# State input product on two column tiles, and the second FP4 quantiser over both token tiles at once

## The chip, the cores and the metric

One Trainium2 chip (trn2), one NeuronCore. The metric is the device time of one launch in microseconds (us), the median of three runs. PE is TensorE, ACT is ScalarE, DVE is VectorE, POOL is GpSimd, SP is SyncE, which issues most transfers here.

## The reference

A residual stream x of 16 sequences of 256 tokens with 128 channels goes through four stages: gated linear attention, a mixture of 8 experts, a state space block, and a feed-forward block with FP4 quantised products. The change touches the last two.

```
# state space block: D_INNER 256, D_STATE 16
xc = silu(conv(xp) + conv_b)
h  = 0.9 * h + 0.1 * (xt @ w_B)          # along the tokens
y  = (h @ w_C) * silu(z);  x = x + y @ w_out
# FP4 block, H 128, I 352, blocks of 16 along the last axis
scale = max(|block|) / 6;  q = nearest grid value of block / scale, times scale
x = x + fp4(silu(fp4(x) @ gate) * (fp4(x) @ up)) @ down
```

## The kernel before, in words

Four phases follow one another: `phase_a` (attention), `phase_b` (router and scatter), `phase_c` (experts, and the preparation of the weights of the last phase), `phase_d` (state space block and FP4 block).

`phase_c` starts with two loads of rows, then SP waits for two memsets of POOL (L1236), issues the loads of the weights (L1240 to L1249) and only then, in order on the same engine, the load of the third group of rows (L1221, in `run_skewed`).

`phase_d` works on one sequence (256 tokens, two token tiles of 128) at a time, in a software pipeline. `body(j)` of each engine holds pieces of several sequences: a = j+3 (projection, convolution, state input, scan), b = j+2 (state output, first FP4 quantiser), c = j+1 (gate and up products, hidden values, second quantiser to its step 4), d = j (last step of the second quantiser, its rescale, the down product), e = j+4 (layer norm). The order on each engine is written by hand, and semaphores join them. Passes j = 0 to 12 have all the sequences a to d; `body` runs from j = -4 to 15, with the passes 1 to 10 in a hardware loop of two passes a turn.

What touches the change, in the order of a pass:

- PE multiplies 128 rows of w_C by the states `hs` (L1744, "state output"), transposes, multiplies `yz` by w_out (L1763), makes the gate and up products, transposes `hq` of token tile 0 into ps_H and of tile 1 into ps_Y (L1788), and then makes the convolution product ps_A (L1796 by the helper's lines 188 to 190) and ps_Z. Then comes the state input product (L1807), `xs` by w_B, two accumulating FP32 matmuls of 128 rows by 16 columns, into ps_M[0:16]; then the down product ps_G (L1816).
- ACT makes `xs` (L1580, two halves), the magnitudes of the second quantiser (L1586, whose operation is at L899; two of 352 elements), `zs` (L1590), the magnitude of the first quantiser (L1593, also L899; 256 elements), and `us` (L1597), the copy of the state input out of PSUM.
- DVE makes step 4 of the second quantiser (L920, `d_fh_sum`, one for each token tile), step 4 of the first (L920, `d_fx_sum`), the scan (L1712) over `us` into `hs`, and later `yz` (L1663), then step 5 of the second quantiser (L921, `d_fh_v`). Steps 0 to 3 (L911 to L917) come in the same pass as the hidden values `hid` (L1691), with the two token tiles taken in turn at each step.
- POOL rescales the two token tiles (L1523, the operation at L895), each as soon as step 5 of its tile is done, and then works out the sums of two layer norms (L1508 to L1515) and gathers rows (L1493).

The class `Fp4` (L876) holds the quantiser's steps: 0 maximum of each block, 1 scale, 2 reciprocal, 3 divide, 4 and 5 rounding by a large constant. `DS` is 16, `N` 256, `F` 352, `P` 128.

Of the kernel before, what the change touches and what calls it, by code (L numbers as in the profile page):

```python
# [28 lines left out]
P = 128  # L29
# [99 lines left out]
def build(nc, io, out):  # L129
    ctx = ExitStack()  # L130
    with ctx:
# [21 lines left out]
        with ExitStack() as mid:  # L153
# [9 lines left out]
            with ExitStack() as early:  # L163
# [14 lines left out]
                "wb": sbm("wb", [P, 2, DS]),  # L178
# [697 lines left out]
class Fp4:  # L876
# [15 lines left out]

    def rescale(self, eng, to):

        return eng.tensor_tensor(self.by(to), self.by(self.v[:, :]), self.spread(self.scale), ALU.mult)  # L895
# [277 lines left out]
def phase_c(nc, io, g):  # L1173
# [3 lines left out]
    with ExitStack() as ctx:  # L1177
# [40 lines left out]
        def _(sp):  # L1218
# [17 lines left out]
            sp.wait_ge(s_zero, 2)  # L1236
# [10 lines left out]
            sp.dma_start(g["wb"][:, :, :], io["L1_attn_w_B"].rearrange("(b p) s -> p b s", p=P)).then_inc(s_w, 16)  # L1247
            sp.dma_start(g["wout"][:, :, :], io["L1_attn_w_out"].rearrange("(b p) s -> p b s", p=P)).then_inc(s_w, 16)
            sp.dma_start(g["wc"][0:DS, :], io["L1_attn_w_C"]).then_inc(s_w, 16)  # L1249
# [3 lines left out]
            sp.wait_ge(s_w, 16 * 7)  # L1253

        @blk_.gpsimd
        def _(pool):
            nc.gpsimd.memset(wraw[:, 2 * D:6 * D], 0.0).then_inc(s_zero, 1)
            nc.gpsimd.memset(g["wc"][:, :], 0.0).then_inc(s_zero, 1)

            pool.wait_ge(s_w, 16 * 7)  # L1260
# [136 lines left out]
def phase_d(nc, io, g, out):  # L1397
# [6 lines left out]
    with ExitStack() as ctx:  # L1404
# [9 lines left out]
        decay = sb("decay", [DS, N])  # L1414
# [11 lines left out]
        us = sb("us", [DS, N])  # L1426
# [10 lines left out]
        hid = sb("hid", [P, 2, F])  # L1437
        hq = sb("hq", [P, 2, F])
        hqT = sb("hqT", [P, 2, 3, P])
        fp4_x = Fp4(nc, sb, "fx", 2 * D)  # L1440
        fp4_h = [Fp4(nc, sb, f"fh{t}", F) for t in range(2)]
# [47 lines left out]
        def _(pool):  # L1489
# [27 lines left out]
            def body(j):  # L1517
                b, d, e = j + 2, j, j + 4
                if live(d):
                    for t in range(2):  # L1520
                        wait(pool, s_qh, d, n=t + 1, per=2)
                        wait(pool, s_hp, d, n=t + 1, per=2, ago=1)
                        fp4_h[t].rescale(nc.gpsimd, hq[:, t, :]).then_inc(s_hq, 1)  # L1523
# [11 lines left out]
        def _(act):  # L1535
# [10 lines left out]
            def body(j):  # L1546
# [35 lines left out]
                if live(c):  # L1582
                    for t in range(2):
                        act.wait_ge(s_qz, c.lin(10, 7 + t))
                        wait(act, s_qh, c, n=t + 1, per=2, ago=1)
                        fp4_h[t].magnitude().then_inc(s_mag, 1)  # L1586
# [7 lines left out]
                if live(a):  # L1594
                    wait(act, s_u, a)
                    wait(act, s_scan, a, ago=1)
                    nc.scalar.activation(us[:, :], ps_M[0:DS, 0:N], ACT.Copy, scale=0.1).then_inc(s_us, 1)  # L1597
# [11 lines left out]
        def _(dve):  # L1609
# [4 lines left out]
            PER = 10  # L1614
# [15 lines left out]
            def hidden_step(c, n, t):  # L1630

                if n == 0:
                    wait(dve, s_h, c, n=t + 1, per=2)
                elif n == 4:
                    wait(dve, s_mag, c, n=t + 1, per=2)
                else:
                    if n == 1:
                        wait(dve, s_hq, c, n=t + 1, per=2, ago=1)
                    dve.wait_ge(s_qz, c.lin(PER, 2 * n - 1 + t))
                fp4_h[t].step(n, hid[:, t, :]).then_inc(s_qz if n < 5 else s_qh, 1)  # L1640
# [16 lines left out]
            def body(j):  # L1657
# [18 lines left out]
                if live(d):  # L1676
                    for t in range(2):
# [169 lines left out]
```

## Time and profile before

| | us |
|---|---|
| median of 3 runs | 649.71 |
| lowest and highest of them | 648.31, 651.97 |
| the profiled execution | 653.99 |
| its span | 652.3 |
| `phase_c`, from its first load to the last product, about | 308 to 415 |
| `phase_d`, about | 419 to 652 |
| PE, DVE, POOL, ACT busy, share of the span | 85%, 67%, 54%, 47% |

The profile is of one execution, whose time is 1.7 us above its span (start and end) and 4.3 us above the median of the runs. Busy time is what an engine spent in instructions; the rows below name an engine, the line in the kernel, the operation, and what goes out and in.

### The profile page before, as it was taken

The numbers are of one execution on the slowest core, as the hardware profiler recorded it, in microseconds if no ns is written. First come the engines' busy times: TensorE is split into PE (matmuls) and PEld (weight loads), VectorE is DVE, ScalarE is ACT, GpSimd is POOL, SyncE is SP. The second block draws the span as 40 slices with busy tenths as digits, with TensorE's granted clock in tenths as the row PEclk, the third lists the DMA queues.
The fourth block names the chain that finished last, engine by engine and source line by source line (L and its number), as shares of the span: only waits on it lengthen the run. The fifth ranks groups of instructions, "written<-read, shape, count | busy, mean of one in ns | idle before, by whom it ended". The sixth has DMA issues, their size and how long they took to land. (4 is left out here: it accounts for less than half of the span.)

```text
span 652.3 us, 15280 instructions
## 1 busy us (share of the span) xinstructions
PE 551.6 (85%) x4468; PEld 445.9 (68%) x4469; DVE 438.3 (67%) x1172; ACT 307.8 (47%) x862; POOL 355.2 (54%) x550
## 2 busy tenths in 40 slices
PE   2799999999999379991799999278899999999965
PEld 1457676776776258871689999266778778778754
DVE  2678999999885155552284343126899899899883
ACT  1356666666574224430245444124545645655632
POOL 4468877878776248885400000445667767764221
PEclk9999999999999659996699999778899999999987
DMA  7000000000004551111422111110011011010000
GB/s 200 16 20 33 19 26 25 16 32 16 23 26 108 158 196 34 32 34 43 116 58 57 56 56 40 33 16 10 10 32 18 16 32 17 16 25 15 10 17 16
DMA packets 41686, 28.12 MB, mean 43 GB/s; under 512 B 5232, under 2 KB 38192, under 8 KB 41648
## 3 DMA queue, kind: packets, MB, share of 16 engines
q1 hardware_dynamic: 36016, 23.46, 12.2%
q0 software_dynamic: 5632, 4.20, 3.7%
q8 instruction: 19, 0.31, 0.2%
q14 instruction: 19, 0.16, 0.1%
HBM read 14.01 MB, written 9.44 MB: 36 GB/s over the span
## 5 line engine op out<-in xcount | busy, mean ns | idle before, releaser
L821 PE MATMUL a_ps_a<-a_qx,a_kt 32*128 32x512 f32 x512 | 70.8, 643 | 1.2 <-DMA a_qx<-a_qs 1.0
L1493 POOL DMA_INDIRECT x<-yg_dram,pos x32 | 58.1, 1815 | 11.9 <-issue 11.9
L895 POOL TENSOR_TENSOR d_hq<-d_fh_v,d_fh_scale 128x352 f32<-128x352 f32 x32 | 27.9, 889 | 57.6 <-DVE d_fh_v L921 57.6
L361 POOL TENSOR_SCALAR_AFFINE_SELECT a_at<-a_at 128x512 f32<-128x512 f32 x80 | 50.5, 650 | 11.8 <-ACT a_at L423 11.5
L1317 DVE TENSOR_TENSOR c_hid<-c_act,c_ps 128x352 f32<-128x352 f32 x40 | 20.7, 520 | 44.4 <-ACT c_act L1274 35.7
L423 ACT ACTIVATE a_at<-a_ps_a 128x512 f32<-128x512 f32 x80 | 44.5, 600 | 11.7 <-PE a_ps_a L821 10.1
L1498 POOL MEMSET d_hs<- 128x256 f32 x1 | 0.3, 311 | 88.3 <-POOLq L1177 88.3
L821 PEld LDWEIGHTS a_ps_a<-a_qx,a_kt 32*128 32x128 f32 x512 | 32.1, 192 | 17.9 <-issue 17.2
L1274 ACT ACTIVATE c_act<-c_ps 128x352 f32<-128x352 f32 x40 | 18.5, 463 | 49.6 <-PE c_ps L190 49.2
L1002 POOL DMA_INDIRECT xg_dram<-xn,pos x32 | 35.3, 1104 | 11.9 <-DVE pos L1091 6.2
L188 PE MATMUL d_ps_A<-d_xnT,wmix 128*128 128x256 f32 x128 | 38.4, 300 | 1.6 <-DVE d_xnT L1672 0.9
L540 DVE TENSOR_TENSOR a_at<-a_ps_a,mask 128x512 f32<-128x512 f32 x48 | 32.7, 684 | 8.6 <-PE a_ps_a L821 7.3
L190 PE MATMUL d_ps_A<-d_xnT,wmix 128*128 128x256 f32 x128 | 37.2, 290 | 0.0
L189 PE MATMUL d_ps_A<-d_xnT,wmix 128*128 128x256 f32 x128 | 37.2, 290 | 0.0
L745 PE MATMUL a_ps_o<-a_at,a_vpad 128*32 128x128 f32 x1024 | 34.6, 276 | 0.0
L1107 DVE TENSOR_TENSOR b_hid<-b_act,b_ps 128x512 f32<-128x512 f32 (+1 forms) x24 | 16.4, 683 | 25.8 <-ACT b_act L1032 25.8
L188 PE MATMUL c_ps<-w13p,c_xT 128*128 x80 | 30.8, 385 | 2.0 <-issue 1.0
L1032 ACT ACTIVATE b_act<-b_ps 128x512 f32<-128x512 f32 (+1 forms) x24 | 14.3, 596 | 38.4 <-PE b_ps L190 37.9
L1367 PE MATMUL c_ps_y<-w,c_hidT 128*128 (+1 forms) x240 | 31.6, 281 | 0.8 <-ACT c_hidT L1291 0.8
L393 POOL TENSOR_TENSOR a_kt<-a_e,a_rope 128x512 f32<-128x512 f32 x16 | 20.4, 1276 | 21.6 <-ACT a_e L447 21.6
L1367 PEld LDWEIGHTS c_ps_y<-w,c_hidT 128*128 128x128 f32 (+1 forms) x240 | 28.3, 191 | 3.0 <-issue 1.9
L1816 PEld LDWEIGHTS d_ps_G<-d_wd,d_hqT 128*128 128x128 f32 (+1 forms) x192 | 23.8, 199 | 8.6 <-issue 5.5
(274 smaller groups left out, 1807.3 us busy)
## 6 DMA issues: line engine op xcount, KB each, us to landing
a_qx<-a_qs SPq DMA_DIRECT2D x64, 64.0 KB, 1.9
b_w<-in_L_ffn_w_eDF_dram SPq DMA_DIRECT2D x2, 1408.0 KB, 8.1
xg_dram<-a_zero SPq DMA_DIRECT2D x40, 64.0 KB, 1.6
c_rows<-xg_dram SPq DMA_DIRECT2D x20, 128.0 KB, 2.1
yg_dram<-c_y SPq DMA_DIRECT2D x20, 128.0 KB, 1.8
out_dram<-x SPq DMA_DIRECT2D x16, 128.0 KB, 1.9
w<-in_L_ffn_w_eFD_dram SPq DMA_DIRECT2D x2, 512.0 KB, 5.1
x<-in_L_attn_x_dram SPq DMA_DIRECT2D x1, 768.0 KB, 5.7
```

What stands on the lines that cost most here:

```text
L188: nc.tensor.matmul(to, left(0), right(0), start=start, stop=False)
L189: nc.tensor.matmul(to, left(0), right(1), start=False, stop=False)
L190: return nc.tensor.matmul(to, left(1), right(0), start=False, stop=stop)
L361: nc.gpsimd.affine_select(at[:, t, r, :, :], at[:, t, r, :, :], pattern=[[0, 4], [1, P]], compare_op=ALU.is_ge, fill=0.0, base=0, channel_ ...
L423: nc.scalar.activation(at[:, t, r, :, :], ps_a[:, r, :, :], ACT.Copy).then_inc(s_copied, 1)
L540: nc.vector.tensor_tensor(at[:, t, r, :, :], ps_a[:, r, :, :], mask[:, 0:1, :].to_broadcast([P, 4, P]), ALU.mult).then_inc(s_masked, 1)
L745: last = nc.tensor.matmul(ps_o[32 * r:32 * r + 32, tile(t)], vpad[:, b.par, t, c0:c0 + 32], at[:, t, r, h, :], start=(t == 0 and h == 0), ...
L821: last = nc.tensor.matmul(ps_a[:, r, :, :], kt[rows, b.par, c_, tile(t)], qx[rows, b.par, :, c_, tile(t)], start=(c_ == 0), stop=(c_ == 1))
L895: return eng.tensor_tensor(self.by(to), self.by(self.v[:, :]), self.spread(self.scale), ALU.mult)
L1002: nc.gpsimd.indirect_dma_start(out=g["xg_dram"][:, :], out_offset=bass.IndirectOffsetOnAxis(ap=g["pos"][:, t:t + 1], axis=0), in_=xn2[:, t ...
L1367: last = nc.tensor.matmul(ps_y[:, t, :], hidT[0:fn, f.par, t, n, :], w2[0:fn, e_out[t], n, :], start=(n == 0), stop=(n == 2))
L1493: nc.gpsimd.indirect_dma_start(out=x[:, t, :], out_offset=None, in_=g["yg_dram"][:, :], in_offset=bass.IndirectOffsetOnAxis(ap=g["pos"][:, ...
```

## The change

The state input product no longer accumulates its two halves of 128 inner channels in the same 16 rows of PSUM. Each half gets its own column tile of the PE array: w_B is kept in 32 columns, of which 16 are zeros, and the halves go to ps_M[0:32] and ps_M[32:64]. `us`, `decay` and the scan work on 64 partitions instead of 16, and w_C stands twice in `wc` (rows 0 to 15 and 32 to 47), so that the state output product adds the halves. For that one more memset on POOL and one more load on SP stand in `phase_c`.

The second quantiser (`fp4_h`) is one of 704 elements instead of two of 352: each of its steps 0 to 5 is one DVE instruction, and its magnitude one ACT instruction. The rescale on POOL stays in two instructions of 352, but both now wait for the one step 5.

```
-                "wb": sbm("wb", [P, 2, DS]),
+                "wb": sbm("wb", [P, 2, 2 * DS]),
...
+    def rescale_part(self, eng, to, c0, c1):
+
+        return eng.tensor_tensor(self.by(to[:, c0:c1]), self.by(self.v[:, c0:c1]),
+                                 self.scale[:, c0 // QB:c1 // QB].unsqueeze(2).to_broadcast([P, (c1 - c0) // QB, QB]), ALU.mult)
...
-            sp.wait_ge(s_zero, 2)
+            sp.wait_ge(s_zero, 3)
...
-            sp.dma_start(g["wb"][:, :, :], io["L1_attn_w_B"].rearrange("(b p) s -> p b s", p=P)).then_inc(s_w, 16)
+            sp.dma_start(g["wb"][:, :, 0:DS], io["L1_attn_w_B"].rearrange("(b p) s -> p b s", p=P)).then_inc(s_w, 16)
             sp.dma_start(g["wout"][:, :, :], io["L1_attn_w_out"].rearrange("(b p) s -> p b s", p=P)).then_inc(s_w, 16)
-            sp.dma_start(g["wc"][0:DS, :], io["L1_attn_w_C"]).then_inc(s_w, 16)
+            for h in range(2):
+                sp.dma_start(g["wc"][2 * DS * h:2 * DS * h + DS, :], io["L1_attn_w_C"]).then_inc(s_w, 16)
...
             nc.gpsimd.memset(g["wc"][:, :], 0.0).then_inc(s_zero, 1)
-
-            pool.wait_ge(s_w, 16 * 7)
+            nc.gpsimd.memset(g["wb"][:, :, :], 0.0).then_inc(s_zero, 1)
+
+            pool.wait_ge(s_w, 16 * 8)
...
-        decay = sb("decay", [DS, N])
+        decay = sb("decay", [4 * DS, N])
...
-        us = sb("us", [DS, N])
+        us = sb("us", [4 * DS, N])
...
-        fp4_h = [Fp4(nc, sb, f"fh{t}", F) for t in range(2)]
+        fp4_h = Fp4(nc, sb, "fh", 2 * F)
...
                 if live(d):
+                    wait(pool, s_qh, d)
                     for t in range(2):
-                        wait(pool, s_qh, d, n=t + 1, per=2)
                         wait(pool, s_hp, d, n=t + 1, per=2, ago=1)
-                        fp4_h[t].rescale(nc.gpsimd, hq[:, t, :]).then_inc(s_hq, 1)
+                        fp4_h.rescale_part(nc.gpsimd, hq, F * t, F * t + F).then_inc(s_hq, 1)
...
                 if live(c):
-                    for t in range(2):
-                        act.wait_ge(s_qz, c.lin(10, 7 + t))
-                        wait(act, s_qh, c, n=t + 1, per=2, ago=1)
-                        fp4_h[t].magnitude().then_inc(s_mag, 1)
+                    act.wait_ge(s_qz, c.lin(5, 4))
+                    wait(act, s_qh, c, ago=1)
+                    fp4_h.magnitude().then_inc(s_mag, 1)
...
-                    nc.scalar.activation(us[:, :], ps_M[0:DS, 0:N], ACT.Copy, scale=0.1).then_inc(s_us, 1)
+                    nc.scalar.activation(us[:, :], ps_M[0:4 * DS, 0:N], ACT.Copy, scale=0.1).then_inc(s_us, 1)
...
-            def hidden_step(c, n, t):
+            def hidden_step(c, n):
 
                 if n == 0:
-                    wait(dve, s_h, c, n=t + 1, per=2)
+                    wait(dve, s_h, c, n=2, per=2)
                 elif n == 4:
-                    wait(dve, s_mag, c, n=t + 1, per=2)
+                    wait(dve, s_mag, c)
                 else:
                     if n == 1:
-                        wait(dve, s_hq, c, n=t + 1, per=2, ago=1)
-                    dve.wait_ge(s_qz, c.lin(PER, 2 * n - 1 + t))
-                fp4_h[t].step(n, hid[:, t, :]).then_inc(s_qz if n < 5 else s_qh, 1)
+                        wait(dve, s_hq, c, n=2, per=2, ago=1)
+                    dve.wait_ge(s_qz, c.lin(5, n))
+                fp4_h.step(n, hid[:, :]).then_inc(s_qz if n < 5 else s_qh, 1)
...
                     for n in range(4):
-                        for t in range(2):
-                            hidden_step(c, n, t)
+                        hidden_step(c, n)
...
-                    nc.vector.tensor_tensor_scan(hs[0:DS, :], decay[:, :], us[:, :], 0.0, ALU.mult, ALU.add).then_inc(s_scan, 1)
+                    nc.vector.tensor_tensor_scan(hs[0:4 * DS, :], decay[:, :], us[:, :], 0.0, ALU.mult, ALU.add).then_inc(s_scan, 1)
...
                     for h in range(2):
-                        last = nc.tensor.matmul(ps_M[0:DS, 0:N], wb[:, h, :], xs[:, h, :], start=(h == 0), stop=(h == 1))
+                        r0 = 2 * DS * h
+                        last = nc.tensor.matmul(ps_M[r0:r0 + 2 * DS, 0:N], wb[:, h, :], xs[:, h, :], start=True, stop=True)
                     last.then_inc(s_u, 1)
```

## Rows read from the trace of the kernel before

**Rows 1.** Page, part 1: busy time, share of the span, instructions.

```profile
PE 551.6 (85%) x4468; PEld 445.9 (68%) x4469; DVE 438.3 (67%) x1172; ACT 307.8 (47%) x862; POOL 355.2 (54%) x550
```

**Rows 2.** Stretches of the last phase: busy us of PE, PEld, DVE, ACT, POOL; clock.

```profile
544.40:618.30 73.90, 69.92 (x481) 59.76 (x481) 67.21 (x206) 40.80 (x115) 41.86 (x64) 1.00 0.10 18
618.30:633.00 14.70, 9.44 (x61) 7.72 (x62) 12.86 (x36) 6.15 (x17) 3.06 (x6) 0.92 0.03 10
```

**Rows 3.** Timeline of PEld in one pass: start, us, idle before and releaser.

```profile
510.09 0.73 PEld L1744 LDWEIGHTS d_ps_Y<-d_hs,wc 128*128 128x128 f32 x4 [0.23 <-DVE d_hs L1712]
...
515.35 0.30 PEld L1788 LDWEIGHTS d_ps_Y<-mask,d_hq 128*128 128x128 f32 x3 [0.19 <-POOL d_hq L895]
```

**Rows 4.** Waits between 475 and 615 us: total, times, longest.

```profile
PEld d_ps_Y L1788 <- POOL d_hq L895: 2.5, 11, 0.3
```

**Rows 5.** Timeline of PE in the same pass.

```profile
507.48 1.04 PE L1807 MATMUL d_ps_M<-d_xs,wb 128*16 128x256 f32 x4 [0.22 <-ACT d_xs L1580]
```

**Rows 6.** Timeline of ACT in the same pass.

```profile
506.59 0.84 ACT L1580 ACTIVATE d_xs<-d_ps_A,cb 128x256 f32<-128x256 f32 x2 [0.52 <-PE d_ps_A L190]
507.32 0.88 ACT L899 ACTIVATE d_fh_k<-d_fh_v 128x352 f32<-128x352 f32 x2
508.09 0.59 ACT L1590 ACTIVATE d_zs<-d_ps_Z 128x512 f32<-128x512 f32 x1
508.57 0.42 ACT L899 ACTIVATE d_fx_k<-d_fx_v 128x256 f32<-128x256 f32 x1
508.88 0.36 ACT L1597 ACTIVATE d_us<-d_ps_M 16x256 f32<-16x256 f32 x1
```

**Rows 7.** Timeline of DVE in the same pass.

```profile
505.31 0.93 DVE L917 SCALAR_TENSOR_TENSOR d_fh_v<-d_hid,d_fh_inv 128x352 f32<-128x352 f32 x2
...
507.85 0.96 DVE L920 SCALAR_TENSOR_TENSOR d_fh_sum<-d_fh_k,d_fh_v 128x352 f32<-128x352 f32 x2 [0.32 <-ACT d_fh_k L899]
509.02 0.42 DVE L920 SCALAR_TENSOR_TENSOR d_fx_sum<-d_fx_k,d_fx_v 128x256 f32<-128x256 f32 x1 [0.22 <-ACT d_fx_k L899]
509.36 0.67 DVE L1712 TENSOR_TENSOR_SCAN d_hs<-d_decay,d_us 16x256 f32<-16x256 f32 x1
...
512.96 0.94 DVE L921 SCALAR_TENSOR_TENSOR d_fh_v<-d_fh_k,d_fh_sum 128x352 f32<-128x352 f32 x2
```

**Rows 8.** Groups of the last phase by line: count, busy us, mean ns.

```profile
L921 DVE SCALAR_TENSOR_TENSOR d_fh_v<-d_fh_k,d_fh_sum 128x352 f32<-128x352 f32 x32 | 15.1, 513 | 0.0
```

**Rows 9.** Timeline of POOL in the same pass.

```profile
503.69 0.72 POOL L1510 TENSOR_TENSOR d_rstd<-d_rstd,halves 128x2 f32<-128x2 f32 x1
...
505.42 0.96 POOL L1510 TENSOR_TENSOR d_rstd<-d_rstd,halves 128x2 f32<-128x2 f32 x1
...
513.55 1.74 POOL L895 TENSOR_TENSOR d_hq<-d_fh_v,d_fh_scale 128x352 f32<-128x352 f32 x2 [1.76 <-DVE d_fh_v L921]
```

**Rows 10.** The rescales on POOL by tile: shortest, median, longest ns.

```profile
L895 POOL TENSOR_TENSOR d_hq<-d_fh_v,d_fh_scale x32: 777/889/1002, 463.7 to 644.3; 128x352 f32<-128x352 f32 x32
```

**Rows 11.** Page, part 5: a product of the first phase on four column tiles.

```profile
L745 PE MATMUL a_ps_o<-a_at,a_vpad 128*32 128x128 f32 x1024 | 34.6, 276 | 0.0
```

**Rows 12.** Timeline of SP at the start of the expert phase.

```profile
314.36 0.47 SPq L1248 DMA_DIRECT2D wout<-in_L_attn_w_out_dram  x1
314.87 0.47 SPq L1249 DMA_DIRECT2D wc<-in_L_attn_w_C_dram  x1
315.38 4.50 SPq L1221 DMA_DIRECT2D c_rows<-xg_dram  x3
```

**Rows 13.** Timeline of PE there.

```profile
319.04 0.44 PE L1359 MATMUL c_ps_t<-mask,c_rows 128*128 128x128 f32 x2 [2.67 <-DMA c_rows<-xg_dram]
```

**Rows 14.** Timeline of ACT in the first pass of the last phase.

```profile
434.65 0.37 ACT L1597 ACTIVATE d_us<-d_ps_M 16x256 f32<-16x256 f32 x1 [0.61 <-PE d_ps_M L1807]
```

**Rows 15.** Timeline of the last pass: the second quantiser of the last sequence.

```profile
640.43 0.93 DVE L917 SCALAR_TENSOR_TENSOR d_fh_v<-d_hid,d_fh_inv 128x352 f32<-128x352 f32 x2
640.96 0.93 ACT L899 ACTIVATE d_fh_k<-d_fh_v 128x352 f32<-128x352 f32 x2 [1.61 <-DVE d_fh_v L917]
641.49 0.96 DVE L920 SCALAR_TENSOR_TENSOR d_fh_sum<-d_fh_k,d_fh_v 128x352 f32<-128x352 f32 x2
...
643.29 1.74 POOL L895 TENSOR_TENSOR d_hq<-d_fh_v,d_fh_scale 128x352 f32<-128x352 f32 x2 [6.65 <-DVE d_fh_v L921]
```

More of the change, by code:

```diff
@@ L1252, in _ @@
                 sp.wait_ge(s_out[par], 16 * (PAIRS // 2))
-            sp.wait_ge(s_w, 16 * 7)
+            sp.wait_ge(s_w, 16 * 8)
         @blk_.gpsimd
@@ L1436, in phase_d @@
         silu = sb("silu", [P, 2, F])
-        hid = sb("hid", [P, 2, F])
-        hq = sb("hq", [P, 2, F])
+        hid = sb("hid", [P, 2 * F])
+        hq = sb("hq", [P, 2 * F])
         hqT = sb("hqT", [P, 2, 3, P])
         fp4_x = Fp4(nc, sb, "fx", 2 * D)
-        fp4_h = [Fp4(nc, sb, f"fh{t}", F) for t in range(2)]
+        fp4_h = Fp4(nc, sb, "fh", 2 * F)
         ps_T, ps_Y, ps_G, ps_U, ps_A, ps_Z, ps_H, ps_M = (bank("ps_" + n) for n in "TYGUAZHM")
@@ L1613, in _ @@
             dve.wait_ge(s_wz, 2)
-            PER = 10
             def norm_stats(j, st, s_stats, s_done):
@@ L1676, in body @@
                 if live(d):
-                    for t in range(2):
-                        hidden_step(d, 5, t)
+                    hidden_step(d, 5)
                 if live(b):
@@ L1690, in body @@
                         wait(dve, s_sg, c, n=t + 1, per=2)
-                        nc.vector.tensor_tensor(hid[:, t, :], silu[:, t, :], (ps_U, ps_Z)[t][:, 0:F], ALU.mult).then_inc(s_h, 1)
+                        nc.vector.tensor_tensor(hid[:, F * t:F * t + F], silu[:, t, :], (ps_U, ps_Z)[t][:, 0:F], ALU.mult).then_inc(s_h, 1)
                         if t == 0 and live(b):
@@ L1695, in body @@
                     for n in range(4):
-                        for t in range(2):
-                            hidden_step(c, n, t)
+                        hidden_step(c, n)
                 elif live(b):
@@ L1704, in body @@
                 if live(c):
-                    for t in range(2):
-                        hidden_step(c, 4, t)
+                    hidden_step(c, 4)
                 if live(b):
@@ L1787, in body @@
                         for f, (f0, fn) in enumerate(FT):
-                            last = nc.tensor.transpose(to[0:fn, P * f:P * f + P], hq[:, t, f0:f0 + fn], ident)
+                            last = nc.tensor.transpose(to[0:fn, P * f:P * f + P], hq[:, F * t + f0:F * t + f0 + fn], ident)
                         last.then_inc(s_hp, 1)
```

## The prediction, made blind

> **What bounds the kernel now.** I read the page first: PE is the busiest engine [rows 1]. Then the last phase by stretches. From 544.40 to 618.30 us six passes go by, 12.3 us each, with PE busy 69.92 of 73.90 us at the full clock [rows 2]. DVE is busy 67.21 us there, so both are nearly full, and what matters is which wait closes each piece of the loop. Two do. First, the state output product starts at 510.09 us, when the scan is done: its weight load had been idle 0.23 us for `d_hs` [rows 3]. Second, the transposes of `hq` of token tile 1 start at 515.35 us, 0.05 us after POOL's rescales end (513.55 + 1.74 = 515.29) [rows 3, 9], and this wait comes 11 times in the steady passes [rows 4]. So the loop runs: `yz` and DVE's queue, step 5 of the second quantiser, POOL's rescales, the transposes, the convolution product, `xs`, then ACT and DVE to the scan, then the state output product and `yz` again. The state input product is not in it: `xs` is done at 507.43 us, and from there ACT works without a gap through `d_fh_k`, `zs`, `d_fx_k` and `us` [rows 6]. The product, started at 507.48 us, is over at 508.52 us [rows 5], 0.36 us ahead of the start of `us` at 508.88 us, and the scan waits in turn for `d_fx_sum`, which waited 0.22 us for `d_fx_k` [rows 7].
>
> **The state input product.** Its four instructions of 256 columns take 1.04 us, 0.24 to 0.26 us each [rows 5]. A product of the first phase on four column tiles has 1024 instructions of 128 columns in 34.6 us of PE time, 34 ns each, though one lasts 276 ns [rows 11]; in turn they would need about half of 0.24 us each. So tiles do overlap. With two tiles I take two rounds of the four, about 0.6 us for the group, 0.43 us less. Bounds: nothing saved, or half of it (0.52 us). In a steady pass the worth is zero, since ACT's queue covers the product by 0.36 us and PE next waits for the scan: what it saves becomes a longer wait before the state output product (0.23 us grows to some 0.6 us). Were that cover gone, it would give 0.43 us a pass. It counts in the first pass, where `us` waited 0.61 us for it [rows 14]: minus 0.43 us, and I give 0.1 us to the second. `us`, scan and memset on more partitions cost what they did: time goes by elements in a partition, the same 256.
>
> **From `xs` to the scan.** ACT's two magnitudes of 352 take 0.88 us and hold `zs` back by 0.77 us [rows 6]. An operation of the same line with 256 elements takes 0.42 us, and one of 352 takes 0.88 - 0.42 = 0.46 to 0.50 us, so about 0.8 ns an element; 704 elements: 0.76 us (0.73 to 0.79). ACT's queue, and `d_fx_k` with it, gains 0.12 us. On DVE step 4 now waits for all of the magnitude. It started at 507.85 us, when the first was done; it will start near 508.12 us (507.32 + 0.76 + 0.04). Two of 352 take 0.96 us [rows 7]. One mean is 0.52 us with 256 elements at 0.42 us [rows 7], so 1.04 ns an element and one of 704 is 0.89 us. It ends at 509.01 us, `d_fx_sum` can start near 508.92 us instead of 509.02, and the scan and the state output product come 0.10 us earlier. Bounds 0 and 0.13 us.
>
> **From step 5 to the transposes.** Before, POOL began on token tile 0 when the first step 5, 0.513 us long [rows 8], was over: 512.96 + 0.51 + 0.08 = 513.55 us [rows 7, 9]. One instruction of 704 takes 0.89 us by the rate above, so POOL begins 0.375 us later, at 513.93 us. The rescales themselves: the pair takes 1.74 us, but a single one between 0.777 and 1.002 us [rows 10], and mean and pair put the long one first (0.99 + 0.78 - 0.03). What differs is that during the first one DVE still has 0.35 us of the second step 5 to go, an operation with both inputs in SBUF. The same shows at L1510, whose form is the same each time: 0.72 us at 503.69 us, and 0.96 us at 505.42 us, when DVE was in L917 (505.31 to 506.24 us), again two inputs from SBUF [rows 7, 9]. After the change nothing of step 5 is left when POOL begins, so I take 0.78 us for both: 1.53 us for the pair, an end at 515.46 us, 0.165 us later than now. Bounds: 0 later, or the whole 0.375 us. Nothing hides it, as the transposes already wait. It hits the 11 steady passes that wait [rows 4].
>
> The Trainium skill has this, page "SBUF — State Buffer", section "Who interferes with whom": a DVE instruction with two SBUF inputs and a GpSimd instruction that reads SBUF share a read interface, and the one that comes second waits for the whole of the first. The rows above agree with it. By the opposite view, that a first rescale after an idle time is slow by itself, the sum would be 0.215 us a pass higher (a rival below).
>
> The same lock now works the other way: L917 becomes one instruction of 0.89 us, and L1510 behind it may end 0.4 us later. That is a norm of a sequence four passes ahead; its `xn` on ACT has over 1 us to spare. Nothing.
>
> **Steps 0 to 3.** Four pairs become four single ones, 0.06 to 0.14 us shorter each, but a step now waits for the one just before it (0.04 us). They end some 0.05 us earlier, and behind them the first quantiser waits for ACT's `xn`. Nothing in a full pass; 0.1 us at pass 13, where DVE alone is the path.
>
> **The tail.** In the last pass the two tiles are what hides latency: the magnitude began at 640.96 us, halfway through step 3, step 4 at 641.49 us, halfway through the magnitude [rows 15]. In one piece: step 3 from 640.42 to 641.31 us, magnitude to 642.09, step 4 to 643.01, the residual addition on DVE (0.25 us), step 5 from 643.26 to 644.15, POOL from 644.23 us instead of 643.29, plus 0.94 us; the faster first rescale gives back 0.22 us. Plus 0.72 us.
>
> **The expert phase.** SP's loads are 0.51 us apart (314.36, 314.87, 315.38 us) and the one more load of w_C stands ahead of the third load of rows [rows 12], for which PE waited 2.67 us [rows 13]. It lands 0.5 us later: plus 0.5 us. The third memset adds perhaps 0.05 us. Bounds 0 and 0.8 us (two small transfers more in a busy queue).
>
> **The sum.** Steady passes: 11 x (0.165 - 0.10) = +0.7. Passes -1, 0 and 12, without the POOL wait: 3 x (-0.10) = -0.3. First passes -0.5, pass 13 -0.1, tail +0.7, expert phase +0.55. Together +1.05, so 653.99 becomes 655.0 us. The median of the runs stands 4.3 us below that execution; on it, 649.7 + 1.1 = 650.8 us. A measurement of this kernel can tell about 0.5% (3.25 us) from no change, so this is no change.
>
> **Rivals.**
> - POOL's first rescale stays at 0.99 us. For it: the last pass, too, has a slow first one after a long idle time (1.74 us for the pair, rows 15), though there, too, DVE was still in step 5. Against: L1510. Then the steady passes give 11 x (0.375 - 0.10) = +3.0 and the tail +0.94: +3.6 in all, 653.3 us, over 0.5% slower. It decides from 0.35 us a pass on. With it goes a longer delay of SP's loads. Chance 0.22.
> - The state input product counts after all. For it: the chain of the page names L1807 and PE, not the scan, and PE is 95% busy. Against: the idle 0.23 us behind `d_hs`. Then 13 full passes give up to 0.43 us each: -5.6 + 1.05 = 645.2 us. Chance 0.15.
> - The two tiles don't overlap, because the two parts of one FP32 matmul stay together or the array must change its division. Then the first passes lose their 0.5 us and nothing else changes: 651.3 us, still no change. Chance 0.1.
> - The clock. PE would be busy some 11.2 of 12.3 us a pass. In the stretch with 9.44 of 14.70 us the granted clock averaged 0.92, in the steady one 1.00 [rows 2]. One fall a turn of the loop would cost over 5 us: 656 us. Chance 0.03.
>
> **How the numbers follow.** The forecast itself has 0.5, and with the third rival 0.6 lies within 0.5%. Slower by over 0.5%: 0.22 + 0.03 = 0.25. Faster: 0.15. The range takes the forecast with its bounds (11 x 0.2 us up, and 2.5 us down from passes that gain more than they lose), the first rival, and most of the way to the second: 646.5 to 654.3 us.
>
> **What would show it.** In the profile after: L1807 at about 0.6 us a group and the wait of PE's weight load before L1744 near 0.6 us; `us` still straight behind `d_fx_k`; L895 with a median of 0.78 us and no long ones; transposes at L1788 waiting for POOL in the same 11 passes; the pass at 12.3 to 12.4 us; the third load of rows 0.5 us later. A pass of 12.6 us or an L895 of 0.99 us would be the first rival; one of 11.9 us, or no wait for `d_hs`, the second.

## The result and the profile after

The median of 10 runs is 654.79 us (651.90 to 657.93), against 649.90 us (648.31 to 652.67) for 10 runs of the kernel before made with them: a ratio of 1.0069, 95% interval 1.0043 to 1.0096. The prediction was 650.8 us, no change, with a range up to 654.3 us. The kernel is slower by about 0.5%, and the prediction was wrong. Two more measurements of the same kernel gave 1.0057 [1.0038, 1.0077] and 1.0040 [1.0017, 1.0063]; their medians were 654.77 and 654.08 us, while those of before stood at 651.38 and 651.12 us. So the change costs 3 to 5 us, 3.7 on the mean of the three.

The profiled execution took 654.48 us (span 652.7 us), only 0.5 us above the one shown of before. The two executions don't say how large the effect is: before's stood 4.1 us above its median, after's 0.3 us below. Single phases can still be compared, and the last one first: from the first `yz` to the last, and from there to the end.

The summary of `yz` by tile (count, shortest, median, longest ns, start of the first and of the last), of before and then of after:

```profile
L1663 DVE TENSOR_TENSOR d_yz<-d_ps_Y,d_zs x16: 690/691/692, 437.0 to 622.1; 128x512 f32<-128x512 f32 x16
```

```profile
L1668 DVE TENSOR_TENSOR d_yz<-d_ps_Y,d_zs x16: 685/692/692, 434.8 to 620.9; 128x512 f32<-128x512 f32 x16
```

The fifteen passes between first and last took 185.1 us and take 186.1 us. What follows the start of the last one, up to the end of the span, took 30.2 us and takes 31.8 us. So in these two executions the loss from the first `yz` on is 2.6 us, and the tail, in which one sequence is alone, has the greater part of it.

Page, part 1, and the two stretches of the last phase (columns as in [rows 2]):

```profile
PE 543.9 (83%) x4468; PEld 442.9 (68%) x4469; DVE 437.2 (67%) x1076; ACT 307.2 (47%) x846; POOL 345.8 (53%) x551
```

```profile
544.40:618.30 73.90, 67.30 (x479) 58.39 (x478) 66.13 (x170) 40.27 (x108) 36.31 (x63) 1.00 0.10 18
618.30:633.00 14.70, 8.45 (x54) 6.71 (x52) 12.07 (x29) 5.01 (x14) 2.85 (x6) 0.96 0.04 11
```

Each engine does less in the same stretch: PE 67.30 us for 69.92, DVE 66.13 for 67.21 with 170 instructions for 206, POOL 36.31 for 41.86. Part of that is the window, which lies a little differently in the pass; but nothing got busier, and still the passes got longer. Less work and more time means longer waits. The waits between 475 and 615 us (total, times, longest), a row of before and then those of after:

```profile
PEld d_ps_Y L1744 <- DVE d_hs L1712: 1.6, 7, 0.2
```

```profile
PE d_ps_Y L1746 <- DVE d_hs L1714: 4.4, 11, 0.5
PEld d_ps_Y L1790 <- POOL d_hq L895: 4.2, 11, 0.4
PEld d_ps_Y L1746 <- DVE d_hs L1714: 3.9, 7, 0.6
```

The wait for POOL's rescale comes 11 times as before, but costs 4.2 us for 2.5 [rows 4]. The wait of the weight load for `d_hs` costs 3.9 us for 1.6. The pass that rows 3 to 9 show, in the timelines of after (start, duration, idle before and releaser), PE and PEld:

```profile
505.55 0.63 PE L1810 MATMUL d_ps_M<-d_xs,wb 128*32 128x256 f32 x4 [0.22 <-ACT d_xs L1587]
```

```profile
508.07 0.73 PEld L1746 LDWEIGHTS d_ps_Y<-d_hs,wc 128*128 128x128 f32 x4 [0.56 <-DVE d_hs L1714]
...
513.49 0.30 PEld L1790 LDWEIGHTS d_ps_Y<-mask,d_hq 128*128 128x128 f32 x3 [0.34 <-POOL d_hq L895]
```

ACT, DVE and POOL:

```profile
505.38 0.79 ACT L904 ACTIVATE d_fh_k<-d_fh_v 128x704 f32<-128x704 f32 x1
...
506.84 0.37 ACT L1603 ACTIVATE d_us<-d_ps_M 64x256 f32<-64x256 f32 x1
```

```profile
506.20 0.89 DVE L925 SCALAR_TENSOR_TENSOR d_fh_sum<-d_fh_k,d_fh_v 128x704 f32<-128x704 f32 x1 [0.57 <-ACT d_fh_k L904]
507.01 0.42 DVE L925 SCALAR_TENSOR_TENSOR d_fx_sum<-d_fx_k,d_fx_v 128x256 f32<-128x256 f32 x1
507.35 0.67 DVE L1714 TENSOR_TENSOR_SCAN d_hs<-d_decay,d_us 64x256 f32<-64x256 f32 x1
509.24 0.69 DVE L1668 TENSOR_TENSOR d_yz<-d_ps_Y,d_zs 128x512 f32<-128x512 f32 x1
510.94 0.88 DVE L926 SCALAR_TENSOR_TENSOR d_fh_v<-d_fh_k,d_fh_sum 128x704 f32<-128x704 f32 x1
```

```profile
511.90 1.54 POOL L895 TENSOR_TENSOR d_hq<-d_fh_v,d_fh_scale 128x352 f32<-128x352 f32 x2 [3.04 <-DVE d_fh_v L926]
```

Three things are to be seen. The product takes 0.63 us for 1.04, and 0.33 of the 0.41 us saved stand again as idle time before the state output product, 0.56 us for 0.23. Of the step from `xs` to the end of the scan, 3.44 us before (506.59 to 510.03), 3.37 are left (504.65, where this pass's `xs` starts, to 508.02). And from the start of `yz` to the end of the rescales it was 4.03 us (511.26 to 515.29) and is 4.20 (509.24 to 513.44), though the pair of rescales fell from 1.74 to 1.54 us.

The tail, DVE, ACT and POOL of the last pass. DVE's rows of before, ahead of those in [rows 15]:

```profile
638.51 0.52 DVE L1691 TENSOR_TENSOR d_hid<-d_silu,d_ps_Z 128x352 f32<-128x352 f32 x1 [0.89 <-ACT d_silu L1560]
638.95 0.94 DVE L911 TENSOR_REDUCE d_fh_amax<-d_hid 128x22 f32<-128x352 f32 x2
639.80 0.37 DVE L913 TENSOR_SCALAR d_fh_scale<-d_fh_amax 128x22 f32<-128x22 f32 x2
640.08 0.43 DVE L915 RECIPROCAL d_fh_inv<-d_fh_scale 128x22 f32<-128x22 f32 x2
```

And of after:

```profile
637.90 0.52 DVE L1695 TENSOR_TENSOR d_hid<-d_silu,d_ps_Z 128x352 f32<-128x352 f32 x1 [1.24 <-ACT d_silu L1567]
638.46 0.89 DVE L916 TENSOR_REDUCE d_fh_amax<-d_hid 128x44 f32<-128x704 f32 x1
639.46 0.19 DVE L918 TENSOR_SCALAR d_fh_scale<-d_fh_amax 128x44 f32<-128x44 f32 x1
639.68 0.43 DVE L920 RECIPROCAL d_fh_inv<-d_fh_scale 128x44 f32<-128x44 f32 x1
640.14 0.89 DVE L922 SCALAR_TENSOR_TENSOR d_fh_v<-d_hid,d_fh_inv 128x704 f32<-128x704 f32 x1
641.06 0.79 ACT L904 ACTIVATE d_fh_k<-d_fh_v 128x704 f32<-128x704 f32 x1 [1.83 <-DVE d_fh_v L922]
641.88 0.89 DVE L925 SCALAR_TENSOR_TENSOR d_fh_sum<-d_fh_k,d_fh_v 128x704 f32<-128x704 f32 x1 [0.85 <-ACT d_fh_k L904]
643.02 0.88 DVE L926 SCALAR_TENSOR_TENSOR d_fh_v<-d_fh_k,d_fh_sum 128x704 f32<-128x704 f32 x1
643.99 1.53 POOL L895 TENSOR_TENSOR d_hq<-d_fh_v,d_fh_scale 128x352 f32<-128x352 f32 x2 [8.14 <-DVE d_fh_v L926]
```

Each engine now waits for the whole of the step before: the magnitude starts 0.92 us after step 3 for 0.53, step 4 another 0.82 us later for 0.53. From the start of the second `hid` to POOL's start it was 4.78 us (638.51 to 643.29) and is 6.09 (637.90 to 643.99). How much of that is the change's doing, the experiments tell.

### The profile page after: what moved, and what is told of

It is laid out like the page before. It is cut to its first block and busy times, and to the rows that moved or that the text cites. A ratio compares the mean times of both kernels' runs of the same rounds, so it can differ in the third digit from the quotient of the medians.

```text
span 652.7 us, 15080 instructions
## 1 busy us (share of the span) xinstructions
PE 543.9 (83%) x4468; PEld 442.9 (68%) x4469; DVE 437.2 (67%) x1076; ACT 307.2 (47%) x846; POOL 345.8 (53%) x551
## 5 line engine op out<-in xcount | busy, mean ns | idle before, releaser
L821 PE MATMUL a_ps_a<-a_qx,a_kt 32*128 32x512 f32 x512 | 69.1, 628 | 1.0 <-DMA a_qx<-a_qs 1.0
L895 POOL TENSOR_TENSOR d_hq<-d_fh_v,d_fh_scale 128x352 f32<-128x352 f32 x32 | 24.5, 786 | 73.0 <-DVE d_fh_v L926 73.0
L1500 POOL DMA_INDIRECT x<-yg_dram,pos x32 | 52.9, 1654 | 11.9 <-issue 11.9
L821 PEld LDWEIGHTS a_ps_a<-a_qx,a_kt 32*128 32x128 f32 x512 | 31.8, 188 | 16.9 <-issue 16.2
```

The lines of the kernel that those rows point to most:

```text
L821: last = nc.tensor.matmul(ps_a[:, r, :, :], kt[rows, b.par, c_, tile(t)], qx[rows, b.par, :, c_, tile(t)], start=(c_ == 0), stop=(c_ == 1))
L895: return eng.tensor_tensor(self.by(to[:, c0:c1]), self.by(self.v[:, c0:c1]), self.scale[:, c0 // QB:c1 // QB].unsqueeze(2).to_broadcast([P ...
L1500: nc.gpsimd.indirect_dma_start(out=x[:, t, :], out_offset=None, in_=g["yg_dram"][:, :], in_offset=bass.IndirectOffsetOnAxis(ap=g["pos"][:, ...
```

## The experiments

In what follows "a pass" is the distance between steady passes (12.34 us before, 12.43 us in the change), "the tail" the time from the start of the last `yz` to the end of the span. The medians of before that were run with the kernels were 651.38, 651.21, 652.20 and 651.12 us (e1 to e4, e5 to e8, e9 and e10, e11 and e12). All kernels compute the whole reference.

### The change again, and its two parts

e1 is the change once more, without an edit. 

> The changed kernel once more, for a second profile. The theory of the waits (the extra time is what the passes of the last phase and its tail show: 0.09 us a pass, 1.6 us in the tail) expects +2 to +2.5 us over the kernel before in the median, a last phase of 239.5 us and a pass of 12.43 us. The theory of the clock (PE's shorter product lets the granted clock fall in some executions) expects +4.5 us again, and profiles that differ from one another by stretches at half clock that are not in the other.

e2 is before with the two column tiles alone: the hunks for `wb`, `wc`, `us`, `decay`, the scan and the extra load; the quantiser stays per token tile.

```diff
-                        last = nc.tensor.matmul(ps_M[0:DS, 0:N], wb[:, h, :], xs[:, h, :], start=(h == 0), stop=(h == 1))
+                        r0 = 2 * DS * h
+                        last = nc.tensor.matmul(ps_M[r0:r0 + 2 * DS, 0:N], wb[:, h, :], xs[:, h, :], start=True, stop=True)
```

> Only the state input product on two column tiles (with its load and its memset in the expert phase); the second quantiser as before. Theory of the waits: a pass of 12.34 us as before, since the product is not in the chain; PE's weight load before the state output product idle for some 0.6 us instead of 0.23; the first passes 0.4 us shorter, the expert phase up to 0.5 us longer: 649.5 to 650.5 us, ratio 0.999 to 1.001. Theory of the clock: 2 to 4 us over the kernel before, with a lower mean granted clock.

e3 is the quantiser alone, on the kernel before.

```diff
-        fp4_h = [Fp4(nc, sb, f"fh{t}", F) for t in range(2)]
+        fp4_h = Fp4(nc, sb, "fh", 2 * F)
```

> Only the second quantiser over both token tiles at once; the state input product as before. Theory of the waits: a pass of 12.43 us, the tail 0.7 to 1.6 us longer: +2 to +2.5 us, ratio 1.003 to 1.004, that is nearly all of what the change costs. Theory of the clock: within 0.2% of the theory of the waits, but less than half of the +4.9 us of the whole change.

Measured: e1 1.0057 [1.0038, 1.0077] (654.77 us), e2 1.0010 [0.9990, 1.0030] (652.37 us), e3 1.0033 [1.0009, 1.0058] (654.31 us). Passes of e1, e2 and e3: 12.43, 12.37 and 12.42 us; tails 31.82, 31.04 and 31.81 us. So the two tiles gain nothing by themselves, to 0.3% in the runs, and the quantiser carries the loss, in the passes and in the tail. e1's +3.4 us lies between its two theories (+2 to +2.5 and +4.5 us) and decides for neither. PEld in e2, the same place in the pass:

```profile
508.54 0.73 PEld L1746 LDWEIGHTS d_ps_Y<-d_hs,wc 128*128 128x128 f32 x4 [0.64 <-DVE d_hs L1714]
```

The wait that [rows 3] show with 0.23 us is 0.64 us there: the product's saving, 0.41 us, has gone into it whole. The second rival, that the product is on the path, falls with this row.

e2 also corrects the reading of the tail. Its quantiser is that of before, and still its tail takes 31.04 us and not 30.18. DVE in that tail:

```profile
637.53 0.52 DVE L1693 TENSOR_TENSOR d_hid<-d_silu,d_ps_Z 128x352 f32<-128x352 f32 x1 [1.24 <-ACT d_silu L1562]
...
640.51 0.96 DVE L920 SCALAR_TENSOR_TENSOR d_fh_sum<-d_fh_k,d_fh_v 128x352 f32<-128x352 f32 x2
641.88 0.42 DVE L1720 TENSOR_TENSOR x<-x,d_ps_G 128x256 f32<-128x256 f32 x1 [0.41 <-PE d_ps_G L1819]
```

In front of step 5 DVE waits 0.41 us for the down product of the sequence before, which in PE's rows of e2 and of before is:

```profile
638.91 2.93 PE L1819 MATMUL d_ps_G<-d_wd,d_hqT 128*128 128x128 f32 x12 [0.63 <-ACT d_hqT L1570]
```

```profile
639.40 1.60 PE L1816 MATMUL d_ps_G<-d_wd,d_hqT 128*128 128x128 f32 x12 [0.77 <-ACT d_hqT L1568]
```

The same twelve matmuls take 2.93 us at a granted clock of 0.50 (1.2 GHz) and 1.60 us at 1.00, as the windows of the two tails have it (637.5 to 643.8 us in e2, 638.5 to 644.3 us in before). From the second `hid` to POOL it is therefore 5.28 us in e2, and in the other two kernels with the old quantiser and this clock (e6, e7) too, where the profile shown of before had 4.78, and so has e8, whose product took 1.60 us. In the change it is 6.09 and 6.07 us (after, e1). Its product ran at the full clock, from 639.28 us for 1.61; at the other it would have been done at 642.21, still ahead of the end of step 4 at 642.77. The quantiser in one piece thus costs 0.8 to 1.3 us here, by the clock that it is compared with.

### What makes the first rescale slow

e4 is the change with step 5 as two instructions again, and POOL released after the first.

```diff
-                    hidden_step(d, 5)
+                    dve.wait_ge(s_qz, d.lin(5, 5))
+                    for t in range(2):
+                        fp4_h.last_step_part(F * t, F * t + F).then_inc(s_qh, 1)
```

> The changed kernel with step 5 of the second quantiser cut into two instructions of 352, and each of POOL's rescales waiting for its own. Theory of the waits: POOL starts 0.37 us earlier again, its first rescale is back at 0.99 us (median of L895 near 0.89 us) because the second half of step 5 runs beside it, the end of the second rescale is where it was before the change, and the pass is 12.34 - 0.07 = 12.27 us: 1 us less over 11 passes than the kernel before; the tail stays 0.5 us or more longer. If the first rescale is slow for another reason than DVE's second input, its median is 0.78 us here and the pass about 12.1 us. Theory of the clock: still 3 us over the kernel before.

Measured: 1.0016 [0.9999, 1.0033] (652.32 us), a pass 12.28 us, the tail 31.68 us. The fifteen passes took 184.3 us for before's 185.1, as expected; the tail lost more than the 0.5 us that were set for it, and the whole lies 0.9 us above before where 0.5 below was expected. The summary by tile of the rescales, of e3 and of e4:

```profile
L895 POOL TENSOR_TENSOR d_hq<-d_fh_v,d_fh_scale x32: 780/786/792, 461.3 to 643.8; 128x352 f32<-128x352 f32 x32
```

```profile
L895 POOL TENSOR_TENSOR d_hq<-d_fh_v,d_fh_scale x32: 777/888/999, 460.0 to 641.0; 128x352 f32<-128x352 f32 x32
```

With nothing left on DVE all 32 last 0.78 to 0.79 us. Cut step 5 in two, and half of them take 1.00 us again as in [rows 10], though POOL is idle ahead of them in both kernels. It is DVE's second step 5 that slows the first rescale, not the idle time before it: the first rival's mechanism falls. It also shows that one instruction, with its faster rescales, is the worse choice: the pair gains 0.2 us, but begins 0.37 us later, 0.15 us a pass.

### The extra load

e5 and e12 are the change with the second load of `w_C` moved behind all of SP's loop, POOL waiting for one load less; e6 is before with that load alone.

```diff
-            for h in range(2):
-                sp.dma_start(g["wc"][2 * DS * h:2 * DS * h + DS, :], io["L1_attn_w_C"]).then_inc(s_w, 16)
+            sp.dma_start(g["wc"][0:DS, :], io["L1_attn_w_C"]).then_inc(s_w, 16)
             run_skewed(sp, body, 0, LO, HI, LAST)
+            sp.dma_start(g["wc"][2 * DS:3 * DS, :], io["L1_attn_w_C"]).then_inc(s_w, 16)
```

> The changed kernel with the second load of w_C moved from ahead of the third load of rows to the end of SP's loop. Theory A (the load ahead of the rows costs PE time in the expert phase, 0.5 us or, with the clock falling for a second stretch there, up to 1.7 us): 0.5 to 1.7 us less than the changed kernel, so a ratio of 1.003 to 1.0045 to the kernel before, and PE's wait for the third rows back at 2.7 us. Theory B (the load costs nothing and the whole change costs what the last phase shows plus chance): ratio 1.0055 to 1.007 as before.

> The kernel before with nothing but the second load of w_C ahead of the third load of rows (into rows of wc that are multiplied by zeros). Theory A: 0.5 to 1.7 us over the kernel before, ratio 1.001 to 1.0025; the last phase unchanged at 12.34 us a pass. Theory B: ratio 1.000.

Measured: e5 1.0042 [1.0022, 1.0061] (654.47 us), e6 0.9996 [0.9968, 1.0024] (651.22 us). e12 was e5 again, and e11 the change again, measured in one set.

> The changed kernel again, side by side with the next one, to settle what the second load of w_C costs ahead of the third load of rows. If it costs 0.5 to 1.5 us: ratio 1.005 to 1.007, 0.001 to 0.0025 above the next one. If nothing: the same ratio as the next one, near 1.004.

> The changed kernel with that load at the end of SP's loop, again. Ratio 1.003 to 1.0045, which is what the last phase alone costs (+2 to +2.9 us). If the load costs something it lies 0.001 to 0.0025 below the one before it, if nothing the two are equal.

Measured: e11 1.0040 [1.0017, 1.0063] (654.08 us), e12 1.0044 [1.0022, 1.0067] (653.97 us). With and without the extra load the time is the same to 0.1 us here, and e6 puts its price at -2 to +1.6 us, around zero. The predicted half microsecond lies inside these intervals: the runs don't show a price, and can't exclude this one. The traces do show the delay. From the first issue of SP for rows to the third there are 8.12 to 8.13 us in the six profiles with the load ahead (after, e1, e2, e4, e6, e11) and 7.66 to 7.68 in the eight without, and PE waits 2.91 to 3.60 us for the third rows (3.25 on the mean) where it waits 2.41 to 3.21 (2.71) without. By the end of the phase nothing of that can be told any more. The expert phase itself, from its first load of rows to the start of the last phase, varies between 106.7 and 108.5 us over the kernels, those with and those without the load. Its stretch from 315 to 323 us (columns as in [rows 2]), of e1 and of e5:

```profile
315.00:323.00 8.00, 6.29 (x25) 5.73 (x26) 0.95 (x2) 2.34 (x8) 6.54 (x4) 0.57 0.07 21
```

```profile
315.00:323.00 8.00, 7.27 (x43) 6.92 (x44) 2.99 (x6) 2.66 (x9) 7.43 (x4) 0.79 0.06 17
```

The granted clock is 0.57 of full speed in the one and 0.79 in the other, so PE spends about 6.9 of these 8 us at 1.2 GHz in e1 and 3.4 in e5. The longer time at 1.2 GHz comes in three of the six profiles with the load (e1, e4, e11) and in one of the eight without (e7 below, whose phase took 108.4 us). Whether the load makes it more frequent these few profiles don't tell; it is a scatter of 1.8 us over which the 0.5 us load can't be seen.

### Taking the product's cover away

If the product is hidden by ACT's queue (the two magnitudes stand ahead of `zs` and `us`), then moving the magnitudes ahead of `xs` must expose it. e7 is before with that order in ACT's stream, e8 is e7 with the two tiles and the late load.

```diff
+                if live(c):
+                    for t in range(2):
+                        act.wait_ge(s_qz, c.lin(10, 7 + t))
+                        wait(act, s_qh, c, n=t + 1, per=2, ago=1)
+                        fp4_h[t].magnitude().then_inc(s_mag, 1)
                 if live(a):
                     wait(act, s_p, a)
...
-                if live(c):
-                    for t in range(2):
-                        act.wait_ge(s_qz, c.lin(10, 7 + t))
-                        wait(act, s_qh, c, n=t + 1, per=2, ago=1)
-                        fp4_h[t].magnitude().then_inc(s_mag, 1)
```

> The kernel before with one edit on ACT: the two magnitudes of the second quantiser stand ahead of xs instead of behind it (the first of them then runs in the 0.5 us in which ACT waits for PE). If the scan is held by ACT's queue, and PE's product stands close behind, the scan comes some 0.7 us earlier and PE, not the scan, now sets the start of the state output product: 0.05 to 0.3 us a pass less, ratio 0.994 to 0.999. If PE's product were already what holds the scan: no change, ratio 1.000.

> The same order on ACT, and the state input product on two column tiles (with the second load of w_C at the end of SP's loop). If the product was only covered by ACT's queue, it now counts: 0.3 to 0.4 us a pass less than with the order alone, a pass of 11.9 to 12.0 us, ratio 0.991 to 0.994. If the shorter product is worth nothing for another reason (the two tiles don't shorten what PE has to do): the same time as with the order alone.

Measured: e7 0.9953 [0.9930, 0.9976] (648.51 us), a pass 12.16 us; e8 0.9858 [0.9825, 0.9891] (642.11 us), a pass 11.76 us. ACT in e7 and, in a fence of its own, in e8:

```profile
500.08 0.87 ACT L899 ACTIVATE d_fh_k<-d_fh_v 128x352 f32<-128x352 f32 x2
500.86 0.81 ACT L1585 ACTIVATE d_xs<-d_ps_A,cb 128x256 f32<-128x256 f32 x2
502.79 0.37 ACT L1597 ACTIVATE d_us<-d_ps_M 16x256 f32<-16x256 f32 x1 [0.34 <-PE d_ps_M L1807]
```

```profile
500.88 0.81 ACT L1587 ACTIVATE d_xs<-d_ps_A,cb 128x256 f32<-128x256 f32 x2
502.42 0.38 ACT L1599 ACTIVATE d_us<-d_ps_M 64x256 f32<-64x256 f32 x1
```

In e7 `us` waits 0.34 us for the product; in e8 it starts without a wait, 1.54 us after `xs` instead of 1.93. The two tiles then give 0.40 us a pass, against nothing in e2: 6.4 us in the medians of the whole kernel, 5.3 us in the profiles between the first `yz` and the last. e7 came as expected. e8's saving over e7 a pass is the expected one, but both its pass and its ratio lie below what was expected (11.9 to 12.0 us, 0.991 to 0.994), as the order alone had given more. e8 is 9.1 us faster than before and the best version found.

e9 is e8 with the quantiser of the change (the whole change, with ACT's order of e7), to see what the quantiser in one piece costs where the product counts.

```diff
-                        fp4_h[t].magnitude().then_inc(s_mag, 1)
+                    fp4_h.magnitude().then_inc(s_mag, 1)
```

> The whole change, with the magnitude of the second quantiser ahead of xs on ACT and the second load of w_C at the end of SP's loop. It differs from the run with that order and the two column tiles alone only in the second quantiser in one piece. Theory of the waits: the end of POOL's second rescale 0.17 us later in each pass, xs up to 0.2 us later behind the one magnitude, which must wait for the whole of step 3, and the tail 1.6 us longer: a pass of 11.95 to 12.15 us and 648 us, ratio 0.994 to 0.997. If the quantiser in one piece costs only as much as it did in the changed kernel (2 to 2.5 us): ratio 0.989 to 0.990.

Measured: 0.9985 [0.9960, 1.0010] (650.96 us), a pass 12.18 us, the tail 31.82 us for e8's 30.54: a miss, since more was lost than expected. In ACT's timeline of e9:

```profile
503.00 0.79 ACT L904 ACTIVATE d_fh_k<-d_fh_v 128x704 f32<-128x704 f32 x1 [0.45 <-DVE d_fh_v L922]
503.70 0.82 ACT L1591 ACTIVATE d_xs<-d_ps_A,cb 128x256 f32<-128x256 f32 x2
```

The magnitude waits for all of step 3 (0.89 us) and holds `xs` back; in e8 it started at half of step 3. The quantiser in one piece costs 0.42 us a pass there, just what the tiles give.

### Only the first steps together

e10 is the change with the late load and with the magnitude, step 4 and step 5 in two parts; only steps 0 to 3 stay in one piece.

```diff
-                    hidden_step(c, 4)
+                    for t in range(2):
+                        wait(dve, s_mag, c, n=t + 1, per=2)
+                        fp4_h.step4_part(F * t, F * t + F).then_inc(s_qz, 1)
```

> The changed kernel with only steps 0 to 3 of the second quantiser in one piece; magnitude, steps 4 and 5 and the rescales go by token tile as before the change (second load of w_C at the end of SP's loop). Theory of the waits: a pass of 12.33 us as before the change; of the 1.6 us that the tail lost, the steps 0 to 3 account for 0.2 to 0.5 us (the tile's reciprocal and the waits between steps) and the three later steps for the rest, so a tail of 30.4 to 30.7 us where the clock goes as before, ratio 0.999 to 1.001. If the tail stays at 31.7 us, the steps 0 to 3 are the cause, ratio 1.002.

Measured: 1.0030 [1.0006, 1.0055] (653.31 us), a pass 12.33 to 12.48 us, the tail 31.53 us: a miss, near the branch in which the first steps are the cause. DVE and ACT in its tail, and POOL:

```profile
640.10 0.89 DVE L933 SCALAR_TENSOR_TENSOR d_fh_v<-d_hid,d_fh_inv 128x704 f32<-128x704 f32 x1
641.03 0.88 ACT L894 ACTIVATE d_fh_k<-d_fh_v 128x352 f32<-128x352 f32 x2 [1.83 <-DVE d_fh_v L933]
...
643.37 1.75 POOL L906 TENSOR_TENSOR d_hq<-d_fh_v,d_fh_scale 128x352 f32<-128x352 f32 x2 [7.71 <-DVE d_fh_v L901]
```

From the second `hid` (637.87 us) to POOL it is 5.50 us here, 6.09 in the change, and 4.78 with the old quantiser at the full clock. DVE doesn't wait for the down product in any of the three, so of the 1.31 us between the last two, steps 0 to 3 in one piece cause 0.72 and the steps behind them 0.59. The 0.72 are two things: step 3 starts 2.23 us after the second `hid` for 1.92, and from there to POOL it is 3.27 us for 2.86, because the first magnitude must wait for the whole of step 3. Merging the first steps, which I had booked as a gain, loses time in the tail, and in the passes it gains nothing.

## Why the prediction was wrong

**What held.** The product: 0.63 us for the predicted 0.6, hidden, its saving turned into the wait for `d_hs` (predicted 0.6 us, 0.56 and 0.64 measured), and worth 0.40 us a pass once the cover is gone (predicted 0.43). The two tiles overlap, so the third rival falls. The single operations: magnitude 0.79 us (0.76), step 4 0.89 (0.89), step 5 0.88 (0.89), both rescales 0.78, the pair 1.54 (1.53). From step 5 to the transposes: 0.17 us later (0.165). `xs` to the scan: 0.07 us earlier (0.10). The rule of the Trainium skill, page "SBUF — State Buffer", section "Who interferes with whom", which I weighed there, is borne out in its direction by e3 and e4: 0.78 us without DVE's instruction, 1.00 with it. In size it isn't: DVE had 0.35 us of step 5 left (512.96 + 0.94 - 513.55), and a wait for all of that would have made the first rescale 1.13 us. The waits before the transposes came in the same 11 passes, and a steady pass grew by 0.09 us where the sum gave 0.065. The granted clock of the steady stretch stayed at 1.00, so the fourth rival falls too.

**What failed: the tail.** The term was +0.7 us, with another -0.1 in pass 13. Every kernel with the whole quantiser in one piece has a tail of 31.81 to 31.83 us. With the old one there are 30.18 (before), 31.04 (e2, e6), 31.03 (e7) and 30.54 us (e8), by how long PE had 1.2 GHz in it: the cost is +0.8 to +1.6 us, 1.05 on the mean of the five. Against e8, whose down product ran at 2.4 GHz as the change's did, it is +1.28. Of that 0.19 lie ahead of the second `hid` (16.98 us from the last `yz`, for 16.78 or 16.79 in e2, e6, e7 and e8), where the sum had the gain of 0.1; 0.32 from there to step 3 (2.24 us for 1.92), where it had nothing; and the rest as predicted: 0.99 from step 3 to POOL (0.94), and 0.22 given back behind it (0.22). The step that failed is thus the sentence "They end some 0.05 us earlier", by which I put step 3 at 640.42 us, where it had been. I had left out that the pairs overlap: in before, a step of token tile 0 starts while the step ahead of it still runs on token tile 1 (639.80 us, where the pair ahead ends at 638.95 + 0.94 = 639.89). In one piece each starts when the one ahead is done, and a little later. From the start of the reduction to step 3 there are 1.68 us (638.46 to 640.14), where it was 1.48 (638.95 to 640.43): 1.00 for 0.85 to the scale, 0.22 for 0.28 to the reciprocal, 0.46 for 0.35 to step 3. Another 0.12 us lie between `hid` and the reduction (0.56 for 0.44). For the reciprocal one instruction is no shorter than the pair: 0.43 us for 44 elements. The group lines of before and after (count, busy us, mean ns):

```profile
L915 DVE RECIPROCAL d_fh_inv<-d_fh_scale 128x22 f32<-128x22 f32 x32 | 7.0, 261 | 0.4 <-DVE d_fh_scale L913 0.3
```

```profile
L920 DVE RECIPROCAL d_fh_inv<-d_fh_scale 128x44 f32<-128x44 f32 x16 | 6.8, 428 | 0.6
```

Two of 22 elements overlapped already: 7.0 us for 16 pairs, 0.44 us a pair. "0.06 to 0.14 us shorter each" was not there for this step. Of the 0.72 us that e10 measures for steps 0 to 3, 0.31 are this loss; the other 0.41, the magnitude's wait for the whole of step 3, stood in the predicted chain.

**What failed: the passes without a wait for POOL.** I gave them -0.1 us each. From the first `yz` to the last there are 15 passes; the sum gave them about +0.4 us, and the profiles have +1.0 to +1.2 (186.1, 186.3 and 186.3 us in three of the change, 185.1 in before and in e6). e2 alone has 185.4 and e3 185.9. The last of the fifteen shows it best: 12.28 us before and 12.29 in e6, 12.45 to 12.46 in the change and 12.43 in e3, so +0.17 where a gain was booked. e10, with only the first steps in one piece, has 12.30: the loss there is that of the magnitude and the steps behind it.

**What stays open: the expert phase.** +0.55 us was read from SP's spacing, and the delay is there: SP's third issue comes 0.46 us later and PE's wait is 0.5 us longer on the mean. But e5, e6, e11 and e12 find no price in the whole, within intervals that hold this one: it is covered by the scatter of the clock.

**The sum.** With the measured terms it is +1.0 to +1.2 in the passes and about +1.05 in the tail. What lies ahead of the first `yz` in the last phase got 0.6 to 1.4 us shorter (the last phase as a whole: 237.5 us before, 239.5, 239.0 and 239.0 in the change; predicted for the first passes: 0.5). That makes about +1 us, where the prediction had +1.05, and by whole phases in single profiles +1.4 to +2.0. The medians say +3.0, +3.4 and +4.9. Of the last figure 1.3 us are in the reference: the same kernel before had a median of 649.9 us with it, and 651.1 to 652.2 us in the later ones. The quantiser alone closes, in a wide interval: e3's ratio is worth +2.1 us (0.6 to 3.8), its passes and tail +1.8 (0.75 and 1.05), and its sum had been about +1.0 (0.7 - 0.3 - 0.1 + 0.7). What the whole change has beyond that, 1 to 2 us, stays open. It is not that before's one profile had a long last phase: e6 is before's code there, and has 238.3 us. What was long in before's profile is what comes ahead of it: its last phase starts at 414.7 us, that of the other thirteen between 411.4 and 413.8.

So two steps failed: the first steps of the quantiser in one piece, booked as a gain of 0.05 us and a loss of 0.2 to 0.3 us in the tail, and the -0.1 us for each pass without a wait for POOL, where the last one has +0.17. The steady pass was costed right to 0.03 us. That the sum by phases still comes near the predicted one is luck: the first passes gained more than was booked, and the half microsecond of the load isn't seen. And a sum of a dozen terms, each known to some 0.3 us, was taken as more certain than it is: it put the kernel 1 us from its reference and far from the 3.25 us that were to count as a change. The chance of 0.25 for slower hung on one rival whose mechanism then fell, and had nothing for the case that came, in which small costs stay and small gains don't.

## What to carry to other kernels

Two tiles that run a few steps apart through DVE, ACT, DVE and POOL are a pipeline. Merging them saved at most 0.1 us a step on the engine here, lost 0.15 and 0.11 us in the tail's reduction and reciprocal, and adds up to half a step at each change of engine; it pays only where an engine is full and nobody waits for the halves. A faster product in the shadow of another engine's queue is worth nothing until that queue is put in another order: the same edit gave 1.001 alone, and 0.40 us a pass after ACT's magnitudes had been moved (from 0.995 with that order alone to 0.986). And when a forecast is a sum of small terms of both signs, the tail, where one sequence is alone, must be worked out from its own rows, and the range must hold the case that the gains fail and the costs don't.

## What was not expected of the hardware

DVE's reciprocal goes by another rate than the operations around it: 0.26 us for 22 elements in a partition, 0.43 us for 44 and, in the first phase, 0.94 us for 128, some 6 to 8 ns an element, where a `scalar_tensor_tensor` takes 0.42 us for 256 and 0.89 us for 704, about 1 ns an element. And the granted clock reaches DVE's path: in the tail the down product takes 1.60 us at 2.4 GHz and 2.93 us at 1.2 GHz, which decides whether the residual addition, and with it step 5 behind it, waits 0.41 us.
